# Perceiver block on one core: seven PSUM copies per pair of batches move from VectorE to ScalarE

## What is computed

```
q = _qdq(x) @ _qdq(wq).T + bq
kv = cond @ wkv.T + bkv
k, v = jnp.split(kv, 2, axis=-1)
attn = jax.nn.softmax(jnp.einsum('bnhd,bmhd->bhnm', q, k) * scale, axis=-1)
o = jnp.einsum('bhnm,bmhd->bnhd', attn, v).reshape(B, N, C)
out = _qdq(o) @ _qdq(wp).T + bp
```

## Time and profile before

| | |
|---|---|
| median of three runs | 2181.81 us |
| the profiled execution, its own time | 2179.32 us |
| its span | 2177.5 us |
| TensorE busy (matmul records) | 2005.8 us, 92% |
| TensorE weight loads | 1569.9 us, 72% |
| VectorE | 1747.0 us, 80% |
| ScalarE | 1610.5 us, 74% |
| GpSimd | 614.7 us, 28% |
| max reductions (L1050), 256 | 468.3 us, 1829 ns each |
| exponentials (L867), 256 | 410.3 us, 1603 ns each |
| value copies on VectorE (L1044), 224 | 145.0 us, 649 ns each |

### The profile page before, as it was taken

How to read it: one execution, slowest core, us unless ns; L and a number is a source line. 1 busy time by engine, 2 the same in 40 slices (tenths; PEclk the granted TensorE clock), 3 DMA queues, 4 the chain that set the end, 5 groups by cost and what they waited for, 6 DMA issues and landing times. The chain is left out here.

```text
span 2177.5 us, 52408 instructions
## 1 busy us (share of the span) xinstructions
PE 2005.8 (92%) x19018; PEld 1569.9 (72%) x19018; DVE 1747.0 (80%) x3649; ACT 1610.5 (74%) x3269; POOL 614.7 (28%) x604
## 2 busy tenths in 40 slices
PE   6999999999999999999999999999997469989966
PEld 5777777777777777777777777777774358878854
DVE  6558898989898989898888889898978747767746
ACT  4778787878787878787878878787877247767743
POOL 0002030303122121313030403030312147767760
PEclk9999999999999999999999999999999579999988
DMA  6888783434334343434343434343421156766738
GB/s 200 284 283 284 238 288 116 140 97 126 117 96 141 73 139 86 130 93 128 94 128 83 137 79 131 82 135 82 139 73 52 62 172 215 218 217 218 221 117 347
DMA packets 189535, 330.04 MB, mean 152 GB/s; under 512 B 37771, under 2 KB 154167, under 8 KB 183136
## 3 DMA queue, kind: packets, MB, share of 16 engines
q1 hardware_dynamic: 170848, 291.99, 44.3%
q0 software_dynamic: 18432, 34.69, 4.3%
HBM read 165.53 MB, written 108.27 MB: 126 GB/s over the span
## 5 line engine op out<-in xcount | busy, mean ns | idle before, releaser
L859 ACT ACTIVATE sb_probsT<-W 128x384 f32<-128x384 f32 (+1 forms) x1024 | 476.7, 517 | 89.5 <-PE W L673 84.6
L1050 DVE TENSOR_REDUCE sb_negmax<-S 128x1 f32<-128x1608 f32 x256 | 468.3, 1829 | 72.3 <-PE S L663 69.6
L867 ACT ACTIVATE sb_probs<-S,sb_negmax 128x1608 f32<-128x1608 f32 x256 | 410.3, 1603 | 92.4 <-DVE sb_negmax L1050 91.6
L673 PEld LDWEIGHTS W<-sb_ident,sb_probs 128*128 128x128 f32 (+1 forms) x3328 | 358.1, 139 | 159.4 <-ACT sb_K_f L851 105.7
L673 PE MATMUL W<-sb_ident,sb_probs 128*128 128x128 f32 (+1 forms) x3328 | 465.1, 278 | 3.9 <-ACT sb_probs L867 2.0
L1440 POOL DMA_INDIRECT y_scratch<-sb_ys,sb_places x256 | 252.1, 985 | 109.3 <-issue 72.5
L851 ACT ACTIVATE sb_K_f<-W,sb_k_cols 128x402 f32<-128x402 f32 x256 | 153.6, 600 | 152.5 <-PE W L636 152.3
L663 PE MATMUL S<-sb_K,sb_Q 32*128 32x402 f32 (+1 forms) x2048 | 243.5, 546 | 13.1 <-ACT sb_probs L867 10.2
L691 PE MATMUL O<-sb_probsT,sb_V 128*32 128x128 f32 (+1 forms) x6656 | 244.1, 277 | 0.0
L549 POOL TENSOR_TENSOR sb_bx<-sb_u,sb_BC 128x512 f32<-128x512 f32 x120 | 172.5, 1459 | 209.2 <-DVE sb_z L1124 190.4
L691 PEld LDWEIGHTS O<-sb_probsT,sb_V 128*32 128x32 f32 (+1 forms) x6656 | 173.5, 109 | 47.4 <-issue 37.3
(11 more groups left out here) (209 smaller groups left out, 3585.1 us busy)
## 6 DMA issues: line engine op xcount, KB each, us to landing
sb_ctx<-ctxT SPq DMA_DIRECT2D x128, 402.0 KB, 4.0
sb_K<-sb_K_f SPq DMA_DIRECT2D x1024, 50.2 KB, 1.9
xe_scratch<-sb_none SPq DMA_DIRECT2D x32, 1088.0 KB, 5.4
sb_xg<-xe_scratch SPq DMA_DIRECT2D x64, 544.0 KB
sb_BC<-bc_scratch SPq DMA_DIRECT2D x32, 1024.0 KB
sb_Q<-sb_q_own SPq DMA_DIRECT2D x128, 128.0 KB, 3.4
y_scratch<-sb_none SPq DMA_DIRECT2D x16, 1024.0 KB, 5.5
sb_rows<-y_scratch SPq DMA_DIRECT2D x16, 1024.0 KB, 8.5
```

The lines of the kernel that those rows point to most:

```text
L673: ins = pe.transpose(W[0:keys_in(t), at * P:(at + 1) * P], probs[n % 2][:, t * P:t * P + keys_in(t)], ident[:])
L859: act.activation(probsT[k][n % (k + 1)][:, 0:wide], ring[bank_of("T", G, k)][:, 0:wide], ACT.Copy)\
L867: act.activation(probs[n % 2][:].rearrange("p (c k) -> p c k", c=QUADS), scores_of, ACT.Exp, bias=negmax[:, slot:slot + 1], accum_out=den[ ...
L1050: dve.tensor_reduce(negmax[:, slot:slot + 1], scores_of, AX.XY, ALU.max, negate=True).then_inc(max_done, 1)
```

## The change

`freed_by` gives the value jobs of the second batch (`job[2] == 1`, slots 2 to 8) to ScalarE; ScalarE gets a `v_up` of its own, called behind the exponential (and behind the softplus exponential, where there is one); VectorE's is called for the first batch only. `times_v` waits for the counter of whichever engine freed the last unit.

```
 def freed_by(job):
-    return "act" if job[0] in ("T", "K") else "dve"
+    return "act" if job[0] in ("T", "K") or job[0] == "V" and job[2] == 1 else "dve"
...
                     if (G - 1) % (2 * STRIPS) == 0:
-                        pe.wait_ge(ring_free["dve"], free_at("V", (G - 1) // SLOTS, step_of(G - 1)[0], len(V_UNITS) - 1))
+                        last = ("V", (G - 1) // SLOTS, step_of(G - 1)[0], len(V_UNITS) - 1)
+                        pe.wait_ge(ring_free[freed_by(last)], free_at(*last))
...
+            def v_up(pair, b, unit):
+                tiles = V_UNITS[unit]
+                act.wait_ge(ring_full, full_at("V", pair, b, unit))
+                if pair > 0:
+                    last = (pair - 1) * SLOTS + (b + 1) * 2 * STRIPS
+                    act.wait_ge(pv_done, max(multiplied_at(n, t) for n in range(last - STRIPS, last) for t in tiles))
+                act.activation(V[b][0:keys_in(tiles[-1]), tiles[0]:tiles[-1] + 1, :].rearrange("p t d -> p (t d)"),
+                                ring[bank_of("V", pair, b, unit)][0:keys_in(tiles[-1]), 0:len(tiles) * D], ACT.Copy).then_inc(ring_free["act"], 1)
...
+                if values_at(G) and values_at(G)[1] == 1:
+                    v_up(*values_at(G))
                 if strip and G % SLOTS not in NO_VALUES:
                     turned(G, 2)
...
-                if v:
+                if v and v[1] == 0:
                     v_up(*v)
```

## The result

The changed kernel takes 2247.9 us (median of 4 runs, 2244.3 to 2248.9) against 2182.7 for the kernel before, run beside it (four runs); the ratio is 1.030, 95% interval 1.029 to 1.0315. It is **slower by 65 us**; the forecast was 2249. The profiled execution has a span of 2247.1 us, 69.6 more than the one before.

A forecast was written before the change was run, and what follows sets the result against it. A three-engine loop, through when ring banks come free, bounds slots 2 to 8. Delays 5.0 minus 0.84 give 4.15 us in 13 pairs (54), plus 14 for three others: +68 on 2181.8, 2249 us; range 2222 to 2275.

The forecast's parts named there:

- What bounds the kernel: Slots 2 to 8: VectorE idle 9.5 of 47.7 us, not scarce; a loop through three engines sets strip length.
- The bound of exponential + 2.24 us: Slots 2 to 8: the job needing the value unit's bank cannot start before exponential + 2.24 us.
- cover of 0.07 us: Slot 4: key unit already starts at exponential + 2.31 us, so the later bank costs no delay.
- Slot 7: VectorE's softplus chain waits for ScalarE's logarithm, now behind the added copy: 0.41 us, taken as 0.5 with a queue.
- Slot 8: Key unit starts 1.62 us later; the turn of the queries no longer waits 0.48; delay 1.14 us.
- The give-back: Slot 9: first scan, stalled by GpSimd whose work is anchored at slot 6, escapes collision; 0.84 us a pair subtracted.
- Busy times: Whole kernel: VectorE's falls by about 72 us, ScalarE's rises by about 64 us.
- A: Slots 5 and 8: VectorE's relief counts, 0.69 us each, 21 us faster, 2161 us; chance 0.03.
- B: Slots after 9 recover 4 us, or the compiled wait does not bind: no change, 2182 us; chance 0.03.
- C: Slot 9 returns the whole 1.76 us, slots 5 to 7 partly covered: 2217 us; chance 0.08.
- D: Slot 7: key unit's delay counts in full, nothing given back; 6.2 us in 13 pairs, 2277 us; chance 0.09.
- the bounds that the prediction set on relief: VectorE's 4.5 us a pair costed at no gain; bounds are nothing and the 0.69 us of slot 8 alone.

The follow-up runs named there:

- experiment 3: Kernel before, with VectorE copying 8 columns instead of 512 of the second batch's value units and nothing going to ScalarE: 2160.7 us.
- experiment 7: Kernel before, first-batch copies on ScalarE ahead of exponential: 2181.1; plus scatter split 2164.8; plus slots 3 to 6 and 8: 2167.1; split, only slots 10, 11, 14: 2168.2.
- experiment 1: Changed kernel with all seven ScalarE copies ahead of the exponential of their strip instead of behind it: 2180.7 us.
- experiment 4: Changed kernel with only the unit of slot 4 on ScalarE: 2182.5 us; with only those of slots 2 and 3: 2212.5 us.
- experiment 6: GpSimd's scatter DMAs split, four ahead of the scan inputs and four behind: kernel before 2169.1 us, changed kernel 2248.3 us.
- experiment 5: Changed kernel with only the unit of slot 8 on ScalarE, behind the exponential: 2204.4 us.
- experiment 2: Kernel before, all copies still on VectorE, but those of slots 2 to 8 wait for the exponential of their strip: 2350.0 us.

## Why the prediction was right

*What bounds the kernel* stood: VectorE's 80% say little of slots 2 to 8. In experiment 3 some 3.4 us a pair of relief bought 1.1, and this came where a bank was free earlier and where the collision shrank; in experiment 7 the relief of five copies bought nothing.

*The bound of exponential + 2.24 us* was measured at 2.22 to 2.24 in slots 2, 3, 5, 6 and 8, and its consequences are within 0.06 us in each of slots 2 to 6. That the place and not the load is the cause is shown by experiment 1, and by slot 4, whose cover of 0.07 us was enough.

*Slot 7*, the guessed term, came to 0.48 (0.5 was taken): the next exponential is late by the added copy. *Slot 8* came to 0.11 more than forecast. Counted from max to max instead the two are 0.24 and 1.57: in slot 8 the exponential no longer follows its max at once (1.86 us after it before, 2.18 now), since ScalarE has a queue there, which is the rest of the term for slot 7.

*The give-back* of 0.84 was taken from one accident in pair 9 and came to 0.86; the collision, its anchor and its limit are shown by experiments 4 and 6. The accident itself was a late transfer of keys, in the kernel before:

```profile
1016.67 0.31 PEld L663 LDWEIGHTS S<-sb_K,sb_Q 32*128 32x128 f32 x8 [1.33 <-DMA sb_K<-sb_K_f]
```

The Trainium skill (SBUF — State Buffer, the section on two separate sides) says that a GpSimd operation that reads SBUF and a VectorE operation with two SBUF inputs lock each other out for a whole instruction. The traces agree: a first scan that starts well before GpSimd's last block is over ends 1.09 us after it (the 2.98 us scan of the earlier trace rows, the 1.80 us scan of pair 9, the 2.45 us scans of experiment 3 and the 1.38 us scans of experiment 1), and one that starts when the blocks are over takes 1.23 us. The scan of the earlier trace rows started within the third of four blocks and waited out the fourth as well. But of the 1.76 us of the stall only 0.86 are had. In experiment 6 the max of slot 10 now waits for its scores, 0.18 us, and slot 10 is longer by 0.46: TensorE is next there, as the forecast read it from pair 9.

*Where the total was lucky.* The sum of the terms, 54 + 14 = 68 us, met 53.8 + 14.7 in the profile. Of the 14.7, 2.5 us lie in slots 0 and 1 of pair 0, ahead of the first moved copy (TensorE's granted clock was at its lower level from 38.7 to 45.4 us there, and at full level in the profile of before), and pair 15 came to 3.5 instead of 4.8; these misses cancel. Of the 53.8, 1.5 us are the clock that pair 6 lost, which no term held. And the medians of the runs differ by 65 us, not by 68. *Busy times* were forecast less well: VectorE's fell by 84 us (72 said) and ScalarE's rose by 49 (64 said).

*The rivals* A to D: A and B are excluded by the result, C and D by the table. Experiment 3 came out at A's 2161, but not by A's reasons. A had 0.69 us in each of slots 5 and 8; slot 5 gained 0.25 and slot 8 nothing, and the rest lay in slot 6, whose wait for the bank went, and in slots 9 and 10. It also exceeds the bounds that the prediction set on relief, nothing to 0.69 us a pair; in the changed kernel, where the bank comes free late, no such gain is seen. What I did not see coming is in the next section but one; it struck the changed kernel in one pair: in pair 6 slot 2 grew by 2.7 us in place of 1.3.

## What to carry to other kernels

When a buffer is read out, its price on the engine matters less than when it comes free for the job that needs it next: find that job in the ring and measure, from the last event ahead of the copy, how late it may be. An engine at 80% of the span can be the wrong one to relieve; cut the profile into its phases, and ask in each who waits for whom. Work that is added to an engine ahead of its long instruction and work added behind it are two different changes: here the one comes out even (0.9 us a pair lost in slots 2 and 7, as much given back in slots 9 and 10) and the other costs 3%.

## What was not expected of the hardware

TensorE can fall to its lower clock level right behind a stop (idle time ahead of its weight loads), and the length of the stop alone does not decide it. In the changed kernel the logits wait 1.60 us in each of pairs 2 to 14; behind one of these 13 stops the clock fell, behind the others it did not. Timeline and window of that pair 6:

```profile
688.82 0.52 PEld L747 LDWEIGHTS W<-sb_gateT,sb_oqT 128*128 128x128 f32 x4 [1.60 <-ACT sb_V L877]
...
692.20 1.72 PE L663 MATMUL S<-sb_K,sb_Q 32*128 32x402 f32 x8
```

```profile
690.70:694.10 3.40, 3.40 (x15) 1.79 (x15) 1.30 (x6) 1.19 (x4) 0.00 (x0) 0.51 0.61 176
```

Eight scores products took 1.72 us at 0.51 of the clock and 0.95 at full clock. With the stop of 2.35 us in slot 8 (experiment 5) the clock fell in 11 of 14 pairs. There slot 8 grew by 2.7 us (median, from exponential to exponential), against 1.25 in pair 14 that kept the clock. The other runs give:

| stop | where | pairs that lost the clock |
|---|---|---|
| 1.60 us | slot 2, changed kernel | 1 of 13 |
| 1.60 us | slot 2, slots 2 and 3 alone (experiment 4) | 1 of 13 |
| 1.60 us | slot 2, changed kernel with the split (experiment 6) | 2 of 13 |
| 1.70 us | slot 7, changed kernel | 0 of 14 |
| 1.82 us | slot 5, experiment 2 | 2 of 14 |
| 1.93 us | slot 2, experiment 2 | 6 of 13 |
| 2.35 us | slot 8, experiment 5 | 11 of 14 |
| 2.41 to 2.54 us | slot 8, experiment 2 | 13 of 13 |

The 1.70 us in slot 7, longer than the 1.60 in slot 2, cost the clock nowhere. What decides besides the length was not tested.
